# Cross-attention block on one core: LayerNorm, bias and mask vectors loaded as rows and turned by TensorE, and loads, casts and stores of the first and last groups in another order

## The reference

```python
x = layer_norm(hidden_states, ln1_w, ln1_b)
q = (x @ q_w + q_b).reshape(B, LQ, H, HD).transpose(0, 2, 1, 3)
k = (encoder_hidden_states @ k_w + k_b) ...
v = (encoder_hidden_states @ v_w + v_b) ...
scores = jnp.einsum('bhqd,bhkd->bhqk', q, k) * scale
scores = jnp.where(mask, scores, mask_value)
out = jnp.einsum('bhqk,bhkd->bhqd', jax.nn.softmax(scores, axis=-1), v)
hidden = out @ cproj_w + cproj_b + residual
y = jax.nn.gelu(layer_norm(hidden, ln2_w, ln2_b) @ fc_w + fc_b, approximate=True)
return hidden + y @ proj_w + proj_b
```

## Time and profile before

| | |
|---|---|
| median of 3 runs | 697.2 us (695.91 to 700.37) |
| profiled execution | 698.95 us |
| its span, first to last instruction | 697.1 us |
| granted TensorE clock, mean | 0.995 |
| busy: PE, DVE, ACT, POOL | 662.5, 496.3, 483.2, 337.5 us |
| DMA | 90.39 MB, 130 GB/s over the span |

### The profile page before, as it was taken

How to read it: one execution, slowest core, us unless ns; L and a number is a source line. 1 busy time by engine, 2 the same in 40 slices (tenths; PEclk the granted TensorE clock), 3 DMA queues, 4 the chain that set the end, 5 groups by cost and what they waited for, 6 DMA issues and landing times.

```text
span 697.1 us, 15066 instructions
## 1 busy us (share of the span) xinstructions
PE 662.5 (95%) x5119; PEld 520.3 (75%) x5119; DVE 496.3 (71%) x1010; ACT 483.2 (69%) x884; POOL 337.5 (48%) x294
## 2 busy tenths in 40 slices
PE   5879899999999999999789999989999999999998
PEld 5778799989989899888656656756766676666664
DVE  5588979978888797879855335978886655764344
ACT  4366966778788777768885676668876667765553
POOL 5185846757567475758665342334412433222121
PEclk9999999999999999999999999999999999999999
DMA  8896745766666576454440332315211311113111
GB/s 238 244 229 174 202 128 148 206 183 193 171 195 189 158 213 190 121 156 126 111 132 24 114 121 63 119 61 182 90 53 40 122 61 43 49 62 121 60 32 61
DMA packets 67934, 90.39 MB, mean 130 GB/s; under 512 B 9752, under 2 KB 38808, under 8 KB 67872
## 3 DMA queue, kind: packets, MB, share of 16 engines
q1 hardware_dynamic: 67600, 89.05, 43.8%
q0 software_dynamic: 272, 0.54, 0.5%
HBM read 68.18 MB, written 20.99 MB: 128 GB/s over the span
## 4 chain that ended last, share of the span: by engine, by line
PE 79%; DMA 6%; issue 4%; DVE 4%; ACT 3%; SPq 2%; POOL 2%; ACTq 0%; DVEq 0%; POOLq 0%
PE psum L1951 8%; PE psum L1949 8%; PE psum L1950 8%; PE psum L1647 6%; PE psum L1649 6%; PE psum L1648 6%; PE psum L1908 5%; PE psum L1910 5%; PE psum L1909 5%; PE psum L1693 4%; PE psum L1677 3%; DMA qk_rows<-qk 2%; PE psum L1798 2%; PE psum L1895 2%; PE psum L1896 2%
## 5 line engine op out<-in xcount | busy, mean ns | idle before, releaser
L660 POOL TENSOR_TENSOR p_lo<-p,p_hi 128x512 f16<-128x512 f32 x128 | 157.4, 1235 | 96.1 <-ACT p_hi L809 91.6
L722 POOL TENSOR_TENSOR w_proj<-w_proj_raw,w_proj 128x512 f16<-128x512 f32 (+1 forms) x64 | 77.2, 1210 | 185.3 <-ACT w_proj_raw L999 146.6
L807 ACT ACTIVATE p<-psum,maskbias 128x512 f32<-128x512 f32 x128 | 87.6, 684 | 19.5 <-PE psum L1677 17.5
L1949 PE MATMUL psum<-w_proj,h_hi 128*128 128x512 f16 (+1 forms) x256 | 98.8, 386 | 0.0
L1951 PE MATMUL psum<-w_proj,h_lo 128*128 128x512 f16 (+1 forms) x256 | 98.0, 383 | 0.0
L1950 PE MATMUL psum<-w_proj,h_hi 128*128 128x512 f16 (+1 forms) x256 | 98.0, 383 | 0.0
L1173 DVE TENSOR_REDUCE negm<-psum 128x2 f32<-128x512 f32 x128 | 83.5, 681 | 17.2 <-PE psum L1693 16.9
L1908 PE MATMUL psum<-y_hi,w_fc_hi 128*128 128x256 f16 x336 | 92.1, 274 | 2.1 <-DVE products L1462 2.0
L1910 PE MATMUL psum<-y_hi,w_fc_lo 128*128 128x256 f16 x336 | 92.1, 274 | 0.0
L1909 PE MATMUL psum<-y_lo,w_fc_hi 128*128 128x256 f16 x336 | 92.0, 274 | 0.0
L809 ACT ACTIVATE p_hi<-psum,maskbias 128x512 f16<-128x512 f32 x128 | 87.7, 685 | 0.0
(11 more groups left out here) (180 smaller groups left out, 1837.3 us busy)
## 6 DMA issues: line engine op xcount, KB each, us to landing
qk_rows<-qk SPq DMA_DIRECT2D x32, 512.0 KB, 3.1
stacks<-qk_rows SPq DMA_DIRECT2D x64, 256.0 KB
w_proj_raw<-in_L_xattn_proj_w_dram SPq DMA_DIRECT2D x64, 256.0 KB, 3.0
stacks<-qk_rows SPq DMA_DIRECT2D x64, 128.0 KB
hidden<-in_x_dram SPq DMA_DIRECT2D x8, 512.0 KB, 4.8
ctx_sb<-in_ctx_dram SPq DMA_DIRECT2D x8, 512.0 KB, 4.1
fc_raw<-in_L_xattn_fc_w_dram SPq DMA_DIRECT2D x16, 256.0 KB, 2.8
fc_raw<-in_L_xattn_fc_w_dram SPq DMA_DIRECT2D x32, 128.0 KB, 3.5
```

The lines of the kernel that those rows point to most:

```text
L660: pool.tensor_tensor(p_lo[:, slot, :], p32[:, u % 2, :], p_hi[:, slot, :], ALU.subtract).then_inc(s["p_lo_done"], 1)
L807: act.activation(p32[:, u % 2, :], psum[:, ST + kc, :], ACT.Exp, bias=maskbias[:, kc:kc + 1], scale=SCALE32)
L1949: nc.tensor.matmul(acc, hi[:, F % 2, i, cut], w[:, 0, :], start=(p == 0 and i == 0), stop=False)
```

## The change

1. The seven vectors are loaded as rows: 4 x 128 or 16 x 128 elements, 512 bytes in a row, into `first_rows` (ln1_w, ln1_b, q_b, k_b) and `second_rows` (ln2_w, ln2_b, fc_b), all issued by ScalarE at its start. TensorE turns each of the two with one transpose (`turn_columns`), the mask with two (`turn_mask`, from `mask_ones`, a float32 copy of the mask that VectorE makes), and VectorE copies them out of PSUM (`take_columns`, `mask_columns`). The eight element-wise loads on SyncE's and GpSimd's queues are gone.
2. SyncE issues the pieces 1 and 2 of q_w and k_w, the second half of v_w, x of batch 1 and the context of batch 1 ahead of `store_mask`, and piece 3 ahead of the first `store_qk`. cproj_w's load stands behind `store_qk` of group 1.
3. ScalarE casts v_w's first half behind `affine_x`, and cproj_w behind `context_hi(0, 1, 1)`, just ahead of `exps` of group 0. GpSimd splits cproj_w behind `low_p` of group 1, and adds cproj_b of batch 0 behind `low_p` of group 0.
4. In `end()`, `store_maxima` of group 30 stands ahead of the first fc_w loads, and GpSimd's last `add_c_bias` behind `low_p` of group 28 rather than 30.
5. `WARM`: 16 idle products at the start (36 before), behind the first transpose, 20 new ones ahead of `project_k`, 15 (19) at the first `transpose_max`.

```diff
-                ("attT", 0, 0): 11, ("begin", 0, 0): 36, ("mT", 0, 0): 19}
+                ("attT", 0, 0): 11, ("begin", 0, 0): 16, ("qkk", 0, 0): 20, ("mT", 0, 0): 15}
...
-            def load_ln1():
-                load_small(cols[:, LN1W:LN1W + KT], column(ln1_w), "ln1_loaded")
-                load_small(cols[:, LN1B:LN1B + KT], column(ln1_b), "ln1_loaded")
-
-            def load_qk_bias():
-                load_small(cols[:, QB:QB + KT], column(q_b), "qkb_loaded")
-                load_small(cols[:, KB_:KB_ + KT], column(k_b), "qkb_loaded")
-
-            def load_mask_columns():
-                load_small(maskcol_raw[:, :], mask.rearrange("b (c p) -> p (b c)", p=P), "maskcol_loaded")
...
             def begin():
                 load_x(0, 0); load_weight_piece(0, 0); load_small(mrow_raw[:, :], mask, "maskrow_loaded"); load_ctx(0, 0)
-                load_weight_piece(1, 0); load_v_half(0); load_ln1(); load_qk_bias(); load_weight_piece(0, 1); load_weight_piece(1, 1)
-                store_mask(); load_weight_piece(0, 2); load_weight_piece(1, 2); load_v_half(1); load_x(0, 1); load_c_weight()
-                store_qk(0, 0); load_weight_piece(0, 3); load_weight_piece(1, 3); fill_stacks(0, 0)
-                store_qk(0, 1); load_mask_columns(); fill_stacks(0, 1)
-                store_qk(0, 2); store_maxima(0, 0); load_ctx(0, 1); fill_stacks(0, 2)
+                load_weight_piece(1, 0); load_v_half(0); load_weight_piece(0, 1); load_weight_piece(1, 1); load_weight_piece(0, 2)
+                load_weight_piece(1, 2); load_v_half(1); load_x(0, 1); load_ctx(0, 1); store_mask(); load_weight_piece(0, 3)
+                load_weight_piece(1, 3)
+                store_qk(0, 0); fill_stacks(0, 0)
+                store_qk(0, 1); load_c_weight(); fill_stacks(0, 1)
+                store_qk(0, 2); store_maxima(0, 0); fill_stacks(0, 2)
                 store_qk(0, 3); load_x(0, 2); fill_stacks(0, 3); store_maxima(0, 1)
                 store_qk(0, 4); store_maxima(0, 2); fill_stacks(0, 4)
                 store_qk(0, 5); fill_stacks(0, 5); store_maxima(0, 3); load_ctx(0, 2)
...
-                store_qk(0, 31); store_maxima(0, 29); fill_stacks(0, 31); load_fc(0); load_fc(1)
-                store_maxima(0, 30); load_proj(0); store_maxima(0, 31); load_fc(2); load_fc(3); load_proj(1); load_proj(2)
+                store_qk(0, 31); store_maxima(0, 29); fill_stacks(0, 31); store_maxima(0, 30)
+                load_fc(0); load_fc(1); load_proj(0); store_maxima(0, 31); load_fc(2); load_fc(3); load_proj(1); load_proj(2)
...
-            def load_columns():
-                for dst, src in ((cols[:, LN2W:LN2W + KT], ln2_w), (cols[:, LN2B:LN2B + KT], ln2_b),
-                                 (cols[:, FCB:FCB + FT], fc_b)):
-                    small(dst, column(src), "mlp_columns_loaded")
+            def load_v_bias():
+                small(vb_bc[:, :], repeated(v_b), "vb_loaded")
+
+            def load_c_bias():
...
-                x_inverse_std(0, 0); split_v_weight(0); load_biases(); split_v_weight(1); x_inverse_std(0, 1); split_c_weight()
-                add_c_bias(0, 0, 0); add_c_bias(0, 0, 1); load_columns()
+                x_inverse_std(0, 0); split_v_weight(0); load_v_bias(); split_v_weight(1); x_inverse_std(0, 1); load_c_bias()
                 low_p(0, 0, 0); low_p(0, 0, 1); low_p(0, 0, 2); low_p(0, 0, 3); x_inverse_std(0, 2)
-                low_p(0, 1, 0); low_p(0, 1, 1); low_p(0, 1, 2); low_p(0, 1, 3)
+                add_c_bias(0, 0, 0); add_c_bias(0, 0, 1)
+                low_p(0, 1, 0); low_p(0, 1, 1); low_p(0, 1, 2); low_p(0, 1, 3); split_c_weight()
...
-                roots(); low_p(0, 28, 0); low_p(0, 28, 1); normalise(0, 6, 0); normalise(0, 6, 1); low_p(0, 28, 2); ln2(1); low_p(0, 28, 3)
+                roots(); low_p(0, 28, 0); low_p(0, 28, 1); normalise(0, 6, 0); normalise(0, 6, 1); low_p(0, 28, 2); ln2(1); low_p(0, 28, 3); add_c_bias(0, 7, 1)
                 low_p(0, 29, 0); low_p(0, 29, 1); low_p(0, 29, 2); low_p(0, 29, 3); ln2(2)
-                low_p(0, 30, 0); low_p(0, 30, 1); low_p(0, 30, 2); low_p(0, 30, 3); add_c_bias(0, 7, 1); ln2(3)
+                low_p(0, 30, 0); low_p(0, 30, 1); low_p(0, 30, 2); low_p(0, 30, 3); ln2(3)
...
+            def by_rows(v):
+                return v.rearrange("(k p) -> k p", p=P)
+
+            for n, v in enumerate((ln1_w, ln1_b, q_b, k_b)):
+                act.dma_start(first_rows[n * KT:(n + 1) * KT, :], by_rows(v)).then_inc(s["rows_loaded"], 16)
             act.wait_ge(s["ident_ready"], 1)
             act.activation(act_scratch[:, :], ident[:, 0:1], ACT.Exp)
+            for rows, v in ((slice(0, KT), ln2_w), (slice(KT, 2 * KT), ln2_b), (slice(2 * KT, 2 * KT + FT), fc_b)):
+                act.dma_start(second_rows[rows, :], by_rows(v)).then_inc(s["second_rows_loaded"], 16)
...
-                        act.wait_ge(s["qkb_loaded"], 32)
+                        act.wait_ge(s["columns_taken"], 1)
...
-                q_weights_hi(0); k_weights_hi(0); context_hi(0, 0, 0); v_weights_hi(0); context_hi(0, 0, 1); affine_x(0, 0)
+                q_weights_hi(0); k_weights_hi(0); context_hi(0, 0, 0); context_hi(0, 0, 1); affine_x(0, 0); v_weights_hi(0)
                 k_weights_hi(1); q_weights_hi(1); x_hi(0, 0); k_weights_hi(2); v_weights_hi(1)
                 qk_high(0, 0); q_weights_hi(2)
                 qk_high(0, 1); q_weights_hi(3); k_weights_hi(3); first_part(0, 0, 0, 0)
-                qk_high(0, 2); c_weights_hi(); maxima_out(0, 0); affine_x(0, 1)
-                qk_high(0, 3); context_hi(0, 1, 0); x_hi(0, 1); first_part(0, 0, 0, 1); mask_columns(0, 0); context_hi(0, 1, 1)
+                qk_high(0, 2); maxima_out(0, 0); affine_x(0, 1)
+                qk_high(0, 3); context_hi(0, 1, 0); x_hi(0, 1); first_part(0, 0, 0, 1); mask_columns(0, 0); context_hi(0, 1, 1); c_weights_hi()
...
+                dve.tensor_copy(mask_ones[:, :], mrow_raw[:, :]).then_inc(s["mask_copied"], 1)
+
+            def take_columns(n):
+
+                dve.wait_ge(s["columns_tr"], n + 1)
+                at, width = ((0, 4 * KT), (4 * KT, 2 * KT + FT))[n]
+                dve.tensor_copy(cols[:, at:at + width], psum[:, MX + n, 0:width]).then_inc(s["columns_taken"], 1)
 
             def mask_columns():
-                dve.wait_ge(s["maskcol_loaded"], 16)
+                dve.wait_ge(s["mask_tr"], 1)
                 dve.wait_ge(s["mask_ready"], 1)
-                dve.tensor_scalar(maskcol[:, :], maskcol_raw[:, :], SCALE32 * MASKED, -SCALE32 * MASKED,
+                dve.tensor_scalar(maskcol[:, :].rearrange("p (b c) -> p c b", c=KC),
+                                  psum[:, MX + 1, 64:64 + B * KC].rearrange("p (c b) -> p c b", c=KC), SCALE32 * MASKED, -SCALE32 * MASKED,
                                   ALU.mult, ALU.add).then_inc(s["mask_ready"], 1)
                 dve.wait_ge(s["mask_ready"], 2)
                 dve.tensor_scalar_add(maskcol[:, :], maskcol[:, :], PSHIFT).then_inc(s["mask_ready"], 1)
...
-                x_statistics(0, 0); q_weights_lo(0); normed_x(0, 0); k_weights_lo(0); mask_row(); context_lo(0, 0, 0); affine_x(0, 0)
-                context_lo(0, 0, 1); q_weights_lo(1); x_lo(0, 0); k_weights_lo(1); k_weights_lo(2); x_statistics(0, 1)
+                x_statistics(0, 0); take_columns(0); q_weights_lo(0); normed_x(0, 0); k_weights_lo(0); context_lo(0, 0, 0); context_lo(0, 0, 1)
+                affine_x(0, 0); mask_row(); q_weights_lo(1); x_lo(0, 0); k_weights_lo(1); k_weights_lo(2); x_statistics(0, 1)
                 low_parts(0, 0); normed_x(0, 1); add_values(0, 0, 0); q_weights_lo(2)
-                low_parts(0, 1); k_weights_lo(3); maximum(0, 0, 0); maximum(0, 0, 1); maximum(0, 0, 2); maximum(0, 0, 3)
-                split_maxima(0, 0); mask_columns(); q_weights_lo(3)
+                low_parts(0, 1); k_weights_lo(3); take_columns(1); mask_columns(); maximum(0, 0, 0); maximum(0, 0, 1); maximum(0, 0, 2); maximum(0, 0, 3)
+                split_maxima(0, 0); q_weights_lo(3)
                 low_parts(0, 2); add_values(0, 0, 1); maximum(0, 1, 0); maximum(0, 1, 1); rest_of_v(0, 0, 0, 0); affine_x(0, 1)
...
-            keep_warm(psum[:, ST, :], "begin", 0, 0)
...
+                if isinstance(G, int) and G == 0 and hh < 2:
+                    pe.wait_ge(s["columns_taken"], hh + 1)
+                    if hh == 1:
+                        pe.wait_ge(s["mask_ready"], 2)
...
-                keep_warm(bank, "qkk", 0, 0)
+                keep_warm(psum[:, ST + 1, :], "qkk", 0, 0)
...
+            def turn_columns(n):
+
+                rows = (first_rows, second_rows)[n]
+                width = (4 * KT, 2 * KT + FT)[n]
+                pe.wait_ge(s[("rows_loaded", "second_rows_loaded")[n]], (4, 3)[n] * 16)
+                nc.tensor.transpose(psum[:, MX + n, 0:width], rows[:, :], ident[0:width, 0:width]).then_inc(s["columns_tr"], 1)
+
+            def turn_mask():
+
+                pe.wait_ge(s["mask_copied"], 1)
```

(7 more changed lines are left out.)

29 lines of the change are left out of this document (12 added, 17 removed).

## The result

The changed kernel takes 703.3 us in the median, the kernel before beside it 697.4: a ratio of 1.0093, 95% interval 1.0067 to 1.012. That is about 6 us slower, inside one per cent by its middle, but outside the predicted range of 690.0 to 700.8. One of its ten executions took 841.1 us at a granted clock of 0.754 and is left out of the ratio. TensorE is busy 662.0 us, as before; what grew is its idle time.

The account below looks back on a forecast made before the run. TensorE was taken as the bound, with winnable idle time only at attention's head and tail. Head +1.8, maxima -2.1 and last addition -1.1 sum to -1.4: 697.2 to 695.8 us, range 690.0 to 700.8.

Parts of the forecast that it names:

- +1.8 for the head: Start of attention up to values(2): a net loss of 1.8 us, bounds 3.0 gained and 5.9 lost.
- First q: TensorE's first q product: starts at 15.6 instead of 16.43 us, a gain of 0.8.
- Scores of group 0, 29.2: TensorE's first scores: start at 29.2 us instead of 31.20, limited by TensorE itself, a gain of 2.0.
- Scores of group 1, a gain of 2.0 (bounds 1 and 3): TensorE's next scores: the 2.0 us gain persists although cproj_w's load, 4.4 us, stands before their fill.
- The cast ahead of the first exponent, 1.9: ScalarE's cast of cproj_w directly before the first exps: takes 1.9 us off the gain of 2.0.
- g: Gain left at the first exponent on ScalarE: taken as 0.5 us, bounds 0 to 1.8.
- GpSimd: GpSimd's queue: additions' lateness vanishes, cproj_w's split delays exps(2, 2) to 70.7 - g; TensorE 1.8 us late, idle time returning some.
- The tail: End of attention: 2.1 us gained by storing maxima first, 1.1 by moving the last addition; 3.2 stay gained.
- The addition's cover: GpSimd's last addition behind group 28: delay costs nothing, hidden by exponents' waits; without that cover 1 us.
- Gain kept: Rival: GpSimd's lateness is absorbed before values(2); head -3.0, tail -3.2, 691.0 us; chance 0.22.
- Slower by slow subtractions: Rival: cproj_w's four subtractions on GpSimd take 2.26 us each, not 1.25; 699.9 us; chance 0.15.
- Tail without effect: Rival: fc_w does not cause the maxima store's 5.2 us, TensorE waits as before; 697.9 us; chance 0.13.

Follow-up runs that it names:

- e4: The kernel before with only the change at the end of attention (point 4); ratio 0.9974 to the kernel before.
- e7: e1 with the old end of attention, leaving only the vectors as rows and the order of the first loads; ratio 0.9989 to the kernel before.
- e8: e1 with GpSimd writing zeros by memset instead of subtracting for v_w's low part; ratio 0.9961 to the kernel before.
- e5: The changed kernel with only cproj_w's load moved back ahead of the first q/k store; ratio 1.0089 to the kernel before.
- e9: e1 with only the two additions of cproj_b late, between GpSimd's groups 0 and 1; ratio 0.9973 to the kernel before.
- e6: The changed kernel with cproj_w's load and cast moved back, GpSimd's additions and subtractions still late; ratio 1.0045 to the kernel before.
- e1: The changed kernel with cproj_w's load, cast and split and the two cproj_b additions back at their old places; 693.2 us, ratio 0.9941 to the kernel before.
- e15: A repeat of e1, the same kernel; 694.2 us, ratio 0.9918 to the kernel before.
- e10: e1 with only cproj_w's four subtractions late, between GpSimd's groups 1 and 2; ratio 1.001 to the kernel before.
- e14: e1 with the cast of v_w's second half moved behind qk_high(0), so GpSimd splits it later; ratio 0.9963 to the kernel before.
- e3: The changed kernel with cproj_w's cast and subtractions and the additions moved back, its load still late; ratio 0.999 to the kernel before.

## Why the prediction was wrong

It forecast 695.8, and the kernel took 703.3. The sum was +1.8 for the head and -3.2 for the tail. The traces show +5 to +6.3 for most of the head (exponents of groups 5 to 28 against the kernel before) and for the tail -3.8 to the last exponent, but only -1.9 to the MLP's start. By the ratios of the changed kernel and of e4, which has its end and the old head, the head lost 8.3 us (+- 2.4) and the end gained 1.8. So two steps failed: the gain of the first loads never came (rows and order give 0.1 +- 0.3% in e7, where 3.0 us were counted on), and GpSimd's lateness, put at 3.3 us, cost 7 to 9.

*First q:* wrong. Starts at 16.63, not 15.6 (16.43 before): VectorE was slower beside GpSimd. In e8, where it was not, it starts at 15.72.

*Scores of group 0, 29.2:* this step failed, with 31.09. It rested on VectorE's wait for x as the only obstacle. That wait did go, but GpSimd's split of v_w now ran beside VectorE's own splits and took 3.1 us from it (3.46 us where the trace of before has 1.29, and 2.20 where it has 1.23). Half of the missing 1.9 us is the first q's lateness (16.63 for 15.6), and 1.11 are a wait in front of the scores; the work between the two was right, 13.35 us where 13.2 + 0.4 were added up. The Trainium skill (SBUF — State Buffer, section "SBUF: two separate sides") states that VectorE's instructions with two SBUF inputs and GpSimd's take a shared port pair as an exclusive lock; I had weighed it for cproj_w's split alone. There the trace shows no price (5.02 us, 4.98 in the earlier trace rows); VectorE's long rows from 66 to 71 us have an input in PSUM, so the rule was hardly put to use. It agrees where I had not looked, at the split of v_w, with the 3.46 for 1.28 us that e8 shows.

*Scores of group 1, a gain of 2.0 (bounds 1 and 3):* failed. Measured +0.5 late. e5 gives 1.4 of it to the megabyte ahead of the fill, which I had put at 4.4 us of transfer and then counted at nothing; the rest is the scores of group 0.

*The cast ahead of the first exponent, 1.9:* right in size (from the scores of group 1 to the first exponent 9.04 us, 7.25 before). With no gain to eat up, it made g = -2.3 instead of +0.5, outside my 0 to 1.8. This is the first mis-sized term: 2.8 us.

*GpSimd:* right in place, and in size up to `values(2)`. Predicted 24.9 us from the first exponent to `exps(2, 2)`, measured 24.25. The additions' lateness is nearly gone by the third `low_p` pair, as said (e9), the subtractions take 1.25 each, and `values(2)` is late by the sum: 76.28, where 74.3 less g is 76.6. Wrong was the last sentence, that idle time later on gives a little back. This is the second mis-sized term. TensorE was to be 1.5 us ahead without GpSimd's lateness and 1.8 behind with it, a price of 3.3; e6 against e1 and e15 puts it at 7 to 9 us. The traces show 3.4 to 4.2 up to `exps(2, 2)` (e10 and e6 against e1), and then 1.8 to 2.8 more between `exps(3, 0)` and `exps(4, 0)`, where TensorE runs at half clock behind its wait. That term stood at nothing in the sum.

*The tail:* -3.2 predicted; -3.8 in the pair of traces up to the last exponent, 2.6 and 3.4 in the two pairs of kernels that differ in it. The 2.1 for the maxima are shown (e4, e7). The 1.1 for the last addition are not shown apart: e7 has the addition in its old place and no wait for the low parts, and no run has this edit alone. Wrong was "so 3.2 us stay gained": 1.8 of them are gone again before the MLP, in e4 as in the changed kernel, with the wait for `hidden` 1.3 us longer. *The addition's cover:* right, no loss is seen behind group 28.

*Rivals.* Gain kept: out, `values(2)` is late. Slower by slow subtractions (699.9): the sign was right and the mechanism wrong, they took 1.25 us each, not 2.26. Tail without effect: out, the wait for the maxima is gone, though only a part of the gain lasts. The rivals that I lacked are the early gain that never comes, and a TensorE that, having waited, runs on at half clock.

*The account.* In the pair of traces: -1.4 forecast, +2.8 for g, +1.7 for the lateness that grew from 4.6 (1.8 + 2.8) to 6.3 at `exps(28, 0)` instead of shrinking, -0.6 for the tail: +2.5, and the last exponent is 2.53 later than before. The table load is 4.38 later (361.18 and 356.80). Of that 2.0 come back in the MLP by an accident of the older trace, whose MLP took 340.30 us with 10 us at a clock of 0.83 from 460 on, and 338.32 without such a stretch in the changed kernel's. So 4.4 of the measured 6 us are seen at the start of the MLP, and 1.5 are in no trace. How much the older trace decides here shows in e4's, which has the same end as the changed kernel: against it the first exponent is 3.2 us late, `exps(4, 0)` 7.0, `exps(28, 0)` 9.9 and the span 8.0 (699.5 and 691.5), where the ratios say 8.3. The times of the changed kernel go with the granted clock: 701.4 us at 0.998, 701.0 to 702.9 at 0.993, 702.1 to 705.5 at 0.990, 708.9 at 0.986. The kernel before has such spread too (0.988 to 0.990 on average), so the mean clock doesn't explain the difference between these two.

## What to carry to other kernels

Before work is moved off a busy start, ask what sets the start: here VectorE's pace beside GpSimd and TensorE's own queue behind the first q, so that nothing was won by moving a megabyte away, and everything by leaving its cast and split where both engines idled (e1, e15: 0.6 to 0.8% faster than the kernel before). A queue whose outputs feed a chain, like GpSimd's `low_p`, pays for each microsecond put in front beyond its own waits, and when TensorE waits for it, the stretch at half clock behind the wait is paid too (1.8 to 2.8 us here). A gain is to be followed to the next stage: the 3.4 us of e4 at the last exponent were 1.6 at the MLP's start. A wait seen in one trace is only a place to put work if it is there in a second trace at full clock.

## What the hardware showed that was not expected

- VectorE's subtraction of 128 x 512 with both inputs in SBUF took 0.64 us a piece alone and 1.73 beside GpSimd's subtraction, and GpSimd's 1.25 became 1.6. With a memset on GpSimd instead, VectorE's took 0.64 again. In e14 the same pair, no longer beside the split, also took 1.28 for two.
- The clock differs by kernel and not only by run. The kernels with cproj_w's work early and the rows turned were granted 0.994 to 0.997 on average in their 9 to 12 runs each (e1, e7, e8, e9, e14, e15; e9 has the additions late), e3 with the load late 0.992, those with GpSimd's subtractions between groups 1 and 2 0.987 to 0.993, the kernel before 0.988 to 0.990. In the windows half clock follows stretches in which TensorE waited (0.63 to 0.89 on average over 10 us); that this makes the difference between the kernels is argued, not tested.
